# Row maxima ahead of the rotary products in VectorE's order, in an attention and MLP block on one core

## The reference, cut to what matters

```
hn = (h - mu) * rsqrt(var + 1e-05) * gamma + beta
q, k, v = hn @ Wq + bq, hn @ Wk + bk, hn @ Wv + bv
q, k = rope(q), rope(k)                     # x * cos + neg_half(x) * sin
attn = softmax(where(causal, q @ k.T / 8, -inf))
x = layernorm(h + (attn @ v) @ Wo + bo + h)
out = layernorm(x + (silu(x @ wg.T) * (x @ wu.T)) @ wd.T)
```

## Time and profile before

| | |
|---|---|
| median of 3 runs | 2231.38 us (2230.36 to 2232.55) |
| profiled execution: its own time | 2229.82 us |
| profiled execution: span | 2228.0 us |
| mean granted TensorE clock | 0.979 of full speed |
| PE busy | 2070.0 us (93% of the span) |
| DVE busy | 1597.6 us (72%) |
| POOL busy | 1391.7 us (62%) |
| ACT busy | 906.6 us (41%) |

### The profile page before, as it was taken

One profiled execution on the slowest core, in us unless ns is written; L12 is line 12 of the kernel. 1 busy time (PEld: TensorE's weight loads), 2 busy tenths in 40 slices (PEclk: granted clock), 3 DMA queues, 4 the chain that ended last, 5 costly groups with the idle time before them and its releaser, 6 DMA issues.

```text
span 2228.0 us, 37497 instructions
## 1 busy us (share of the span) xinstructions
PE 2070.0 (93%) x14720; PEld 1287.2 (58%) x14720; DVE 1597.6 (72%) x2262; ACT 906.6 (41%) x1245; POOL 1391.7 (62%) x1204
## 2 busy tenths in 40 slices
PE   6779999999999989999999999999999989889997
PEld 5445555555555545555555555555555545789996
DVE  8576878686878776767777777778787763556654
ACT  4424443444444434434343434343434345434342
POOL 1457777777787866677767777878787879000000
PEclk9899999999999999999999999999999999999999
DMA  6311212121202122122111212121112131231300
GB/s 223 119 30 38 62 39 62 39 62 39 58 25 68 42 68 72 45 65 63 48 53 43 58 43 58 43 58 34 48 34 58 29 119 48 67 104 57 112 10 29
DMA packets 116149, 132.16 MB, mean 59 GB/s; under 512 B 15248, under 2 KB 71184, under 8 KB 115728
## 3 DMA queue, kind: packets, MB, share of 16 engines
q1 hardware_dynamic: 115984, 129.92, 19.5%
HBM read 56.47 MB, written 39.85 MB: 43 GB/s over the span
## 4 chain that ended last, share of the span: by engine, by line
PE 60%; DVE 24%; DMA 5%; SPq 4%; issue 4%; ACT 1%; POOL 1%; ACTq 0%; DVEq 0%
PE o_ps L1239 13%; DVE mpart L833 9%; PE m_ps L1184 7%; DMA rot<-qr 5%; PE s_ps L1205 4%; SPq L385 4%; PE s_ps L1209 4%; PE s_ps L1207 4%; PE s_ps L1211 4%; PE x_ps L1139 3%; DVE qr L860 3%; PE x_ps L1246 3%; DVE qc L871 2%; PE gu_ps L1139 2%; PE gu_ps L1140 2%
## 5 line engine op out<-in xcount | busy, mean ns | idle before, releaser
L542 POOL TENSOR_TENSOR acc<-acc,pt 128x512 f32<-128x512 f32 (+3 forms) x1024 | 1195.8, 1200 | 228.0 <-ACT pt L591 228.0
L591 ACT ACTIVATE pt<-s_ps 128x1024 f32<-128x1024 f32 (+3 forms) x640 | 544.8, 895 | 704.8 <-PE s_ps L1211 342.4
L833 DVE TENSOR_REDUCE mpart<-m_ps 128x2 f32<-128x1024 f32 (+2 forms) x576 | 624.9, 1085 | 288.2 <-PE m_ps L1184 215.7
L1239 PE MATMUL o_ps<-pt,v 128*64 128x512 f32 (+3 forms) x2560 | 547.5, 549 | 0.0
L1184 PE MATMUL m_ps<-qk 64*128 64x512 f32 (+3 forms) x1280 | 290.0, 449 | 85.0 <-DVE mpart L833 73.7
L1184 PEld LDWEIGHTS m_ps<-qk 64*128 64x128 f32 x1280 | 121.1, 185 | 395.6 <-DVE mpart L833 223.6
L1239 PEld LDWEIGHTS o_ps<-pt,v 128*64 128x64 f32 x2560 | 157.8, 138 | 239.1 <-issue 213.8
L537 POOL TENSOR_TENSOR acc<-pt 128x512 f32<-128x512 f32 (+1 forms) x128 | 161.7, 1283 | 193.7 <-ACT pt L591 193.7
L1205 PE MATMUL s_ps<-qk 64*128 64x512 f32 (+3 forms) x1280 | 253.7, 392 | 0.0
L1209 PE MATMUL s_ps<-qk 64*128 64x512 f32 (+3 forms) x1280 | 235.6, 363 | 0.0
L1211 PE MATMUL s_ps<-aux,ones_r 64*128 64x512 f32 (+3 forms) x1280 | 234.7, 362 | 0.0
(11 more groups left out here) (165 smaller groups left out, 2882.0 us busy)
## 6 DMA issues: line engine op xcount, KB each, us to landing
rot<-qr SPq DMA_DIRECT2D x512, 64.0 KB, 2.0
attn<-o_sum SPq DMA_DIRECT2D x64, 256.0 KB, 2.3
o_raw<-attn SPq DMA_DIRECT2D x8, 2048.0 KB, 8.9
v<-v_far SPq DMA_DIRECT2D x16, 768.0 KB, 5.2
v_far<-v_part SPq DMA_DIRECT2D x48, 256.0 KB, 2.0
w_raw<-in_wqkv SPq DMA_DIRECT2D x34, 128.0 KB, 5.1
v_far<-v SPq DMA_DIRECT2D x16, 256.0 KB, 2.4
v<-v_far SPq DMA_DIRECT2D x16, 256.0 KB, 5.0
```

What stands on the lines that cost most here:

```text
L542: nc.gpsimd.tensor_tensor(sums, sums, probs, ALU.add).then_inc(summed, 1)
L591: nc.scalar.activation(pt[:, u % SLOTS, :, q0:NB], s_ps[:, two:two + 2, q0:NB], ACT.Exp, scale=SCALE)\
L833: nc.vector.tensor_reduce(dst, m_ps[:, :, 0:w], AX.X, ALU.max, negate=True).then_inc(maxed, 1)
L1239: last = nc.tensor.matmul(o_ps[rows, q0:NB], v[par][:, j, rows], pt[:, u % SLOTS, a, q0:NB], start=(j == 0), stop=(j == n - 1), skip_group ...
```

## The change: one unit of maxima ahead of the two products

In a group that follows a projected piece, DVE takes the first unit of the group's row maxima before the two products of that piece, instead of after them. The second unit and all else keep their order. `early` is 0 in pass 0, and where a tile of values stands at the end of the group before: PE then waits for the products before it makes the group's first unit. In the groups that follow no piece, and in pass 15, the order is what it was.

```diff
                     if ended is not None:
                         turn_sums(it - 1 if g == 1 else it, ended)
+                    ms = group_maxima(kind, g)
+                    late = 2 if kind is not FIRST else len(ms)
+
+                    early = 0 if kind is FIRST or (g - 1, 1) in V_PIECES[it] else 1
+                    for m in ms[:early]:
+                        maximum(it, m) if m < NM else maximum(it + 1, m - NM)
                     if g - 1 in PIECE and kind is not LAST:
                         products(it + 1, *PIECE[g - 1], 1 - par, 2)
-                    ms = group_maxima(kind, g)
-                    late = 2 if kind is not FIRST else len(ms)
-                    for m in ms[:late]:
+                    for m in ms[early:late]:
                         maximum(it, m) if m < NM else maximum(it + 1, m - NM)
```

## The result

The changed kernel takes 2351.9 us (median of 4 runs, 2348.34 to 2359.97) against 2231.97 us beside it: a ratio of 1.0545 (95% interval 1.0523 to 1.0568), 120 us slower. The profiled execution took 2348.57 us.

The account below looks back on a forecast made before the run. PE, 96% busy in passes 1 to 14, was taken to bound the kernel. Waits of 115 us and 20 us of clock on the profiled 2229.8 us made 2365, with the median 1.6 us higher at 2366; range 2315 to 2400.

Parts of the forecast that it names:

- groups 4 and 5: K0's projection loses 0.34 us and group 5's transpose starts 2.95 later, in 13 passes: 38.4 us.
- groups 8 and 9: Addition and third maximum move by 2.22 us, so PE's first unit of group 9 comes 2.2 later, 12 passes: 26.4 us.
- groups 10 and 11 (K1 and the transpose): Group 11's narrow maximum with a transpose behind it, 4 us; K1's addition in group 9, 3 us.
- groups 14 to 19, passes without value pieces: In passes 4, 5, 12, 13 and 14, later additions delay PE by 5.6 us a pass: 28 us.
- groups 14 to 19, passes with value pieces: Value projections wait for `qc` in groups 14, 16 and 18, 0.5 us a place in 8 passes: 12 us.
- passes 6 and 7 elsewhere: Their remaining places, put between a gain of 2 and a loss of 6: 4 us.
- `qr` starts a chain that ends last: `qr`, its rotation DMA, the addition and DVE's queue behind it often end last, so a later `qr` delays PE.
- The rival of direct waits: PE loses only where it waits for `qc`, the rotated halves still being early enough: 45 us, 2276 us; chance 0.09.
- The clock: Some 40 new waits, 5/12 of them followed by a clock fall at 1.2 us each: 20 us, bounds 0 and 68.
- The rival of no falls: The clock stays up and only the waits count: 2231.4 + 115 = 2346 us; chance 0.19.
- Faster: PE's second units wait less for the first maximum: 4 us in group 9, 8 us together, 2223 us; chance 0.03.
- The signs: `qc` 2.6 us after group 4's unit; waits 2.8 (group 5's transpose), 2.3 (group 9); passes 4, 5, 12-14 grow 11 to 12.

Follow-up runs that it names:

- e4: All 107 groups in the order sine product, first maximum, cosine product, so the rotation's DMAs start as in the kernel before: 2237.08 us, 1.0027 of the kernel before.
- e1: The kernel before with the first maximum ahead of the products in group 4 alone (13 passes): 2244.98 us, a ratio of 1.0060.
- e3: The kernel before with the first maximum ahead of the products in groups 14, 16 and 18 alone: 2292.1 us, a ratio of 1.0264.
- e5: The kernel before (old order) with POOL's sums cut to 32 columns of each block, row sums left incomplete: 2140.44 us, a ratio of 0.9606.
- e6: The changed kernel (new order) with the same cut of POOL's sums to 32 columns: 2285.92 us, 145 us above the old order with that cut.
- e7: The kernel before with the products moved to the head of the group, ahead of the spread: 2200.02 us beside 2227.87, a ratio of 0.9878.
- e2: The kernel before with the first maximum ahead of the products in group 5 alone (14 passes): 2257.65 us, a ratio of 1.0122.

## Why the prediction was right, and where its sizes were off

Forecast 2366 us, in a range of 2315 to 2400; measured 2351.9. The direction, the mechanism and the order of size held. That the time came within 14 us is in part luck: the waits are 92.9 us instead of 115 and the clock 27.1 instead of 20, and the terms of the waits miss in both directions. The measured column is PE's idle time in passes 1 to 14, after less before, from PE's first unit of the first group named to that of the group behind the last:

| term | forecast, us | measured, us |
|---|---|---|
| groups 4 and 5 | 38 | 29.7 |
| groups 6 and 7 | not in the sum | -9.1 |
| groups 8 and 9 | 26 | 14.6 |
| groups 10 and 11 (K1 and the transpose) | 7 | 9.2 |
| groups 14 to 19, passes without value pieces | 28 | 29.9 |
| groups 14 to 19, passes with value pieces | 12 | 18.1 |
| passes 6 and 7 elsewhere | 4 | in the rows above, 0.5 beside them |
| sum | 115 | 92.9 |

- **What bounds the kernel.** Right. DVE got 34 us less busy and the kernel 120 us slower: PE's waits decide, not DVE's load.
- **`qr` starts a chain that ends last.** Right, and the core of it. The wait for the rotation rose by 151 us. The distance from the end of `qr` to the addition stayed near 3.85 us in most places (3.83 to 4.0 for 49 of the 76 additions that waited before, and for 79 of 107 now, in passes 1 to 14; the others take up to 5.8), and e4 brings nearly everything back by starting the rotation in time. The rival of direct waits (45 us) falls with the result itself, with e1 and with e3.
- **Groups 4 and 5,** 2.95 us a pass forecast: 2.24 in pass 13. The projection's shift was right: 0.36 (1685.79 - 1682.65 against 1594.97 - 1592.19), 0.34 forecast. What was mis-sized is the `spread` behind the addition, taken at its old length of 0.97: it took 0.16, here and in 11 other of the 14 passes. And a term is missing: in group 6 PE already stood 13.0 us in all before the second unit, and the later transpose used up 10.0 of it; the sum put that at nothing.
- **Groups 8 and 9,** 2.2 us forecast: 1.24 in pass 13. The addition did move by 2.2, but "the third maximum behind it too" failed: the addition shrank from 1.69 to 0.69 (on average over passes 1 to 14 the addition of this group went from 1.58 to 0.78). This is the largest mis-sized term.
- **The common cause of both** is that the prediction took the lengths of DVE's operations as fixed. In e5 and e6, with POOL nearly idle, the addition takes 0.70 and 0.69 us on average, against 1.09 in the kernel before.
- **How POOL's sums set these lengths.** The trace of the kernel before shows it. All 85 additions that began with 0.15 us or more of one of POOL's sums still to run ended 0.55 us after that sum (0.547 to 0.555), and the 32 that began with POOL idle took 0.67 to 0.69 us. All 60 spreads that began during one of POOL's sums ended 0.03 to 0.04 us after it, and the three that began with POOL idle took 0.17 to 0.18. The changed kernel shows the same (all 53 such additions, all 34 such spreads). So the change moved these operations to other points of POOL's sums. The spread of group 5 and the addition of group 8 came out shorter; the additions of groups 16 and 18 came out longer (1.19 to 1.40 and 0.74 to 1.21 us on average). The prediction had read no row of POOL that could tell. The Trainium skill (SBUF — State Buffer, section Who interferes with whom) says that a VectorE instruction with two SBUF inputs contends with a GpSimd instruction that reads SBUF, and one with at most one SBUF input, outside the two-port modes, does not. The traces agree: the additions, with two SBUF inputs, vary, and the products, which read one input from PSUM, took 0.73 to 0.75 us throughout. With POOL nearly idle the new waits come to 116.6 us, near the forecast's 115, but only as a sum: groups 4 and 5 cost 29.5 there too.
- **The clock,** 20 us forecast with bounds of 0 and 68: PE's busy time grew by 27.1 us. The rival of no falls is out. The granted clock was 0.5 from the last microsecond of waits of 2.58 and 2.08 us on, and between the waits of 1.6 us or more in that stretch there are at least 4.6 us, longer than any of them (the longest is 3.5). The Trainium skill (TensorE: Matmul & The Clock Gate, section HAM oscillation) blames idle gaps that are longer than the work between them; the trace does not agree, and the measurement decides. The number of falls was well met, 17 more where 40 x 5/12 makes 16.7, but by two misses: the changed kernel has 38 waits of 1.6 us or more, 26 more than before and not 40, and 22 falls beside them, a larger share than 5 of 12. What the price missed is that a fall can last 6.8 us instead of 3.4, as four do.
- **Groups 14 to 19.** Forecast 28 us for the passes without value pieces and 12 for the others. e3 has the three groups alone. Its windows for passes 1 to 14:

```profile
219.00:1853.50 1634.50, 1520.16 (x11020) 857.75 (x11018) 1179.91 (x1482) 640.04 (x854) 1184.37 (x1037) 0.98 0.17 48
```

The stretch is 66.4 us longer than before, PE's idle time 114.3 instead of 68.4 us: 45.9 for waits against 40 forecast, and 20.5 for the clock, which the forecast had for the whole change. In group 19 the changed kernel meets the 2.0 forecast (1.83 in four of the five passes) by luck: two misses cancel. The addition took 1.39 to 1.44 in those four, where the forecast took 0.78, and the spread 0.16, where the forecast took 0.97 (in the kernel before it took 1.25 at that place).
- **Faster.** The mechanism was not empty, but small: in e4, which keeps it, PE's idle time in group 9, its place, falls by 2.7 us, where 4 were put. The larger fall of the waits for maxima there, 15 us, is mostly group 6, where it is only group 5's wait moved.
- **The signs.** `qc` ended 2.58 us after group 4's unit (2.6 forecast), and passes 4, 5, 12, 13 and 14 grew most, by 8 to 17 us (11 to 12 forecast), the others by 3 to 8. The transpose of group 5 waited 2.12 us instead of 2.8, and the first unit of group 9 0.79 instead of 2.3; both misses are for the most part the shorter spread and the shorter addition.

## What to carry to other kernels

When the order of two operations on one engine is changed, follow each of them to its last consumer: here the one with a DMA and 3.85 us or more behind it had to go first, and the reduction, which the next engine needed only after more work of its own, could wait. Work that fits into a gap before an operand arrives should stay there; putting the operation that waits for the operand first turns the gap into idle time. And a new wait on TensorE costs more than its length when the clock falls after it.

## What was not expected

- POOL's sums cost far more than the lengths of DVE's additions: with them cut to 32 columns the kernel before takes 2140 us, 4% less, and PE's idle time in passes 1 to 14 is 14.4 us instead of 68.4. DVE is busy 152 us less in those passes, more than its additions and spreads gave up in the whole run (96 us), and the clock does not fall once there. Which of these the time comes from was not tried.
- Ahead of the spread, the products won 28 us in e7 where 8 to 15 were expected, from a move of 0.97 us in two groups of each pass. Of the 31 us that its passes 1 to 14 gained, some 10 are the transpose's wait for the cosine product, which the expectation had not counted.
- The clock took more than the waits in e2 (16.4 against 8.8 us).
- The length of an addition is decided by POOL's sum in flight: while that sum runs, a start 1 us later makes the addition 1 us shorter, and a start just behind the beginning of the next sum makes it long again (1.8 us in rows of the changed kernel).
